# A transformer block on one core: the six middle batches of the attention stage written out one by one, instead of a loop on the engines

## The chip, the core and the metric

The kernel runs on one core of a Trainium2 chip. The metric is the device time of one execution, in microseconds. Five engines work on their own instruction streams and meet at semaphores: TensorE (PE: matmuls, with their weight loads as PEld), VectorE (DVE), ScalarE (ACT), GpSimd (POOL) and SyncE (SP), which here only starts transfers.

## What is computed

A "macaron" block: half of a mixture-of-experts layer, causal attention, and half of the same mixture again, each on a normalised input and added to x.

```
x = x + 0.5 * ffn(layernorm(x))       # x: 8 batches x 1024 tokens x 256
x = x + attn(layernorm(x))            # 16 heads of 16, causal softmax, output projection + bo
x = x + 0.5 * ffn(layernorm(x))
# ffn: top-2 of 8 experts per token; an expert whose count exceeds its capacity of 1280
#      tokens is dropped as a whole, and its tokens get nothing from it
```

The kernel works out the gate and the counts, and enters the expert code (`moe_experts`, from L527) only if an expert is within its capacity. In the trace it is jumped over both times, so both ffn parts come down to gates and counts.

## The kernel before

**Stages.** A short stage computes gates and counts for all 8192 tokens (to 94 us of the span). Then comes attention, to 1534 us, batch after batch, and behind it the second count.

**The attention of a batch** is four steps, one for each group of four heads (`hg` 0 to 3). A step runs over 12 groups of keys and queries with 4 heads each, 48 units. Per unit PE makes one transposed score tile (`st`, L1146), ACT takes its exponential into `probs` (L817), POOL masks the diagonal ones (`affine_select`, L668), and PE multiplies `probs` with the values into `o_bank` (`pv`, L1178). Beside that, 15 units ahead, the row maxima of the next step are found: PE makes score tiles in the other orientation (`s`, L1159) in three PSUM banks in turn, and DVE reduces each one. A tile on the diagonal is reduced together with the causal mask by `tensor_tensor_reduce` (L966, two instructions on DVE: the operation and the read of its accumulator into `max_diag`), a full one by `tensor_reduce` (`max_full`, L970). PE may write a bank again only when `max_done` says that DVE has taken its maximum. The maxima are split into three bf16 parts (`mfin`, L977 to L987, each after a drain), transposed by PE (L1131) and copied by ACT into `q_stack` (L804).

**Around the units** lies other work at fixed unit numbers (`PLACE`, a table written by hand): projections for later steps (`misc`, L1104, with a split into three bf16 parts by ACT, POOL and DVE), values (L1099), transposes of outputs, output projection (L1125), normalisation of the next batch's x (`lnstat` L449, `lnnorm` L458) and the gate of the last one. SP writes the parts to DRAM and reads them back as stacks.

**The order.** `step_plan` makes one list of events, and each engine's program goes through the same list and emits what is its own. The lists are in five sections (`make_sections`): prologue, batch 0, batches 1 to 6, batch 7, epilogue. `walk` (L269) goes through them. A section that occurs once is written out with constants. The section that occurs six times (`times` is 6) is emitted once inside `eng.Fori`, a loop that runs on each engine with the batch number `b` in a register, and the count that a wait compares with is then worked out from the register: `lin(b, k, c)` is `b * k + c`, and `n(...)` does the same for counts of a kind of event.

```
with eng.Fori(b0, b0 + times) as b:
    events(b)
```

**The increments.** `passed(eng, name)` (L438) follows certain waits on SP, POOL and DVE. It increments a semaphore that nobody waits for:

```
eng.wait_ge(s_full, lin(b, NU * NG, NU * (hg + ahead) + u + 1))
if diag:
    passed(eng, "vector")
```

The wait is then carried by the instruction that increments, and the operation comes behind it.

## Time and profile before

| | |
|---|---|
| median of three runs | 1573.51 us (1569.27 to 1577.14) |
| the profiled execution, its own time | 1577.63 us |
| its span, from first to last instruction | 1575.9 us |
| gates and counts, to | 94 us |
| prologue (maxima and projections of batch 0) | 94 to 183 us |
| batch 0, written out | 183 to 327 us |
| batches 1 to 6, looped | 327 to 1376 us |
| batch 7, written out | 1376 to 1534 us |
| epilogue and second count | to 1576 us |
| mean granted clock of TensorE | 0.936 of full speed |
| busy share | PE 85%, DVE 72%, ACT 62%, POOL 26% |

The profile is of one execution, 4.1 us above the median. PE's clock is granted at full speed (2.4 GHz, written 1.00) or at half of it (1.2 GHz); a window's figure between 0.5 and 1 is the mean of the two. "Idle before <-" names what ended an engine's wait. "issue" is idle time that no semaphore ended.

### The profile page before, as it was taken

What the parts mean: (1) busy time and instruction counts of PE and PEld (TensorE: products, weight loads), DVE (VectorE), ACT (ScalarE), POOL (GpSimd) and SP (SyncE); (2) the same over time, 40 slices, a digit from 0 to 9 for tenths busy, and PEclk for the clock granted to TensorE, in tenths of its full rate; (3) what the DMA queues carried; (4) which work ended last, traced back from release to release, by engine and by line L of the source; (5) the groups of instructions that cost most, each with busy time, mean ns of one, the idle gap of its engine ahead of it and who ended that gap; (6) DMA issues with size and microseconds to landing.
All of it is one profiled execution on the core that took longest, in us unless ns stands there. A gap on an engine that the chain in (4) does not pass through costs nothing.

```text
span 1575.9 us, 32770 instructions
## 1 busy us (share of the span) xinstructions
PE 1344.9 (85%) x8464; PEld 581.0 (37%) x8464; DVE 1127.1 (72%) x3677; ACT 977.3 (62%) x1729; POOL 413.3 (26%) x536
## 2 busy tenths in 40 slices
PE   3645799999988899989988898989998998999874
PEld 2422233344433443344333343344433443344332
DVE  6723788777876778767877777767886777768642
ACT  5411377766666667756666767757765766666751
POOL 2311223223321232223321232223322232222110
PEclk9866799999998999999999999999999999999985
DMA  7022412222322222312322232202322232221000
GB/s 243 1 46 60 112 35 61 61 61 61 81 59 63 46 59 72 74 33 61 88 59 55 53 82 62 62 26 61 88 61 53 60 80 61 63 53 40 5 1 27
DMA packets 53969, 95.75 MB, mean 61 GB/s; under 512 B 5776, under 2 KB 47376, under 8 KB 47632
## 3 DMA queue, kind: packets, MB, share of 16 engines
q1 hardware_dynamic: 51744, 92.29, 23.5%
q8 instruction: 83, 1.36, 0.4%
q10 hardware_dynamic: 2032, 1.19, 0.3%
q14 instruction: 110, 0.90, 0.2%
HBM read 59.91 MB, written 33.55 MB: 59 GB/s over the span
## 4 chain that ended last, share of the span: by engine, by line
PE 61%; DVE 12%; issue 11%; ACT 9%; DVEq 3%; DMA 2%; POOL 2%; ACTq 0%; SPq 0%; POOLq 0%
PE o_bank L1178 15%; PE s L1159 14%; PE st L1146 12%; PE misc L1104 7%; PE misc L1125 4%; PE misc L1099 3%; ACT q_stack L804 3%; PE misc L510 3%; DVE s L966 3%; ACT probs L817 2%; DVE max_full L970 2%; ACT parts L780 1%; DVE stats L449 1%; DVE xn L458 1%; DMA part_dram<-parts 1%
## 5 line engine op out<-in xcount | busy, mean ns | idle before, releaser
L817 ACT ACTIVATE probs<-st 128x512 f32<-128x512 f32 (+1 forms) x1216 | 632.3, 580 | 248.6 <-PE st L1146 128.5
L966 DVE CUSTOM_DVE_ANT_0 s<-s,causal 128x128 f32<-128x128 f32 (+3 forms) x1024 | 494.8, 504 | 239.3 <-PE s L1159 221.1
L1159 PE MATMUL s<-k_stack,q_stack 96*128 96x512 bf16 (+3 forms) x1536 | 507.6, 341 | 58.2 <-DVE max_diag L966 32.8
L1146 PE MATMUL st<-q_stack,k_stack 108*128 108x512 bf16 (+3 forms) x1536 | 499.8, 338 | 37.9 <-ACT probs L817 19.6
L970 DVE TENSOR_REDUCE max_full<-s 128x1 f32<-128x512 f32 x512 | 350.1, 684 | 32.5 <-PE s L1159 32.1
L1178 PE MATMUL o_bank<-probs,v_aug 128*17 128x512 f32 (+3 forms) x3072 | 332.7, 506 | 16.5 <-ACT parts L780 10.7
L668 POOL TENSOR_SCALAR_AFFINE_SELECT probs<-probs 128x512 f32<-128x512 f32 x256 | 164.6, 645 | 584.7 <-ACT probs L817 584.1
L1159 PEld LDWEIGHTS s<-k_stack,q_stack 96*128 96x128 bf16 x1536 | 150.4, 99 | 446.6 <-DVE max_diag L966 200.7
L1146 PEld LDWEIGHTS st<-q_stack,k_stack 108*128 108x128 bf16 x1536 | 151.2, 99 | 158.9 <-ACT probs L817 67.2
L804 ACT ACTIVATE q_stack<-misc 12x2048 bf16<-12x2048 f32 x64 | 119.7, 1870 | 77.4 <-PE misc L1131 76.7
L680 POOL TENSOR_TENSOR rest<-qk,parts 128x512 f32<-128x512 f32 x64 | 74.1, 1159 | 356.4 <-ACT parts L780 347.0
L1104 PE MATMUL misc<-x_t,w_qk 128*128 128x512 f32 x256 | 132.1, 641 | 21.9 <-issue 13.4
L966 DVE DVE_READ_ACCUMULATOR2_ANT max_diag<- 128x1 f32 x1024 | 144.3, 141 | 0.2
L780 ACT ACTIVATE qk<-misc,qk_bias,qk_scale 128x512 f32<-128x512 f32 x64 | 49.8, 777 | 139.2 <-PE misc L1104 123.7
L1178 PEld LDWEIGHTS o_bank<-probs,v_aug 128*17 128x17 f32 x3072 | 51.4, 96 | 142.4 <-issue 97.5
L686 POOL TENSOR_TENSOR parts<-rest,parts 128x512 bf16<-128x512 f32 x64 | 74.7, 1167 | 58.0 <-DVE parts L1010 58.0
L449 DVE BATCH_NORM_STATS2 stats<-x_all 128x6 f32 (+1 forms) x184 | 72.3, 419 | 10.5 <-issue 5.2
L458 DVE TENSOR_SCALAR xn<-x_all,mean_var,rstd 128x256 f32 (+1 forms) x152 | 64.1, 439 | 16.3 <-POOL rstd L465 13.8
L1104 PEld LDWEIGHTS misc<-x_t,w_qk 128*128 128x128 f32 x256 | 48.9, 202 | 64.4 <-issue 47.6
L1125 PE MATMUL misc<-w_o,o_t 128*128 128x256 f32 x256 | 67.2, 408 | 5.2 <-ACT parts L780 4.2
L1099 PE MATMUL misc<-w_v,x_t 128*128 128x256 f32 x256 | 65.0, 399 | 4.7 <-ACT parts L780 2.6
L1028 DVE TENSOR_TENSOR x_all<-misc,x_all 128x512 f32 (+1 forms) x32 | 22.1, 692 | 51.2 <-PE misc L1125 51.2
(107 smaller groups left out, 931.9 us busy)
## 6 DMA issues: line engine op xcount, KB each, us to landing
part_dram<-parts SPq DMA_DIRECT2D x128, 192.0 KB, 2.8
q_stack<-part_dram SPq DMA_DIRECT2D x32, 384.0 KB
k_stack<-part_dram SPq DMA_DIRECT2D x32, 384.0 KB
x_all<-x SPq DMA_DIRECT2D x16, 512.0 KB, 5.7
q_stack<-part_dram SPq DMA_DIRECT2D x32, 256.0 KB
k_stack<-part_dram SPq DMA_DIRECT2D x32, 256.0 KB
out<-x_all SPq DMA_DIRECT2D x8, 1024.0 KB, 17.1
q_stack<-part_dram SPq DMA_DIRECT2D x32, 128.0 KB
```

The source lines that it names most:

```text
L449: nc.vector.bn_stats(stats[:, t, :], x_tiles(tile, 1)[:, 0, :])
L668: nc.gpsimd.affine_select(out=now, in_=now, compare_op=ALU.is_ge, fill=0.0, base=0, pattern=[[0, HG], [1, P]], channel_multiplier=-1)\
L804: nc.scalar.activation(q_stack[rows, hm, :, c * CW:(c + 1) * CW], misc[rows, :].rearrange("p (o c) -> p o c", o=1) .to_broadcast([MROWS, H ...
L817: nc.scalar.activation(probs[:, g % 2, h - part:h + 1, 0:width], st_bank[i % 3][:, 0:share * width] .rearrange("p (h c) -> p h c", c=width ...
L966: nc.vector.tensor_tensor_reduce(out=bank, in0=bank, in1=causal[:, CW - width:CW], scale=1.0, scalar=-BIG, op0=ALU.add, op1=ALU.max, accum ...
L970: nc.vector.tensor_reduce(max_full[:, (hg + ahead) % 2, h, ib - CT:ib - CT + 1], bank, AX.X, ALU.max)\
L1099: last = nc.tensor.matmul(misc[:, t * D:(t + 1) * D], x_t[:, dc, t0:t0 + P], w_v[:, dc, :], start=dc == 0, stop=dc == DC - 1)
L1104: last = nc.tensor.matmul(misc[:, :], w_qk[:, dc, hq, :], x_t[:, dc, c * CW:(c + 1) * CW], start=dc == 0, stop=dc == DC - 1)
L1125: last = nc.tensor.matmul(misc[:, t * D:(t + 1) * D], o_t[:, dc, t * P:(t + 1) * P], w_o[:, dc, :], start=dc == 0, stop=dc == DC - 1)
L1146: score = nc.tensor.matmul(st_bank[i % 3][:, part * width:(part + 1) * width], k_stack[0:KROWS + MROWS, hg, h, jb * P:(jb + 1) * P], q_sta ...
L1159: nc.tensor.matmul(s_bank[u % 3][:, 0:width], q_stack[0:KROWS, hm, h, ib * P:(ib + 1) * P], k_stack[0:KROWS, hm, h, j0:j0 + width], start= ...
L1178: last = nc.tensor.matmul(o_bank[32 * h:32 * h + VW, off:CW], v_aug[:, jb, of % NG * HG + h, :], probs[:, g % 2, h, 0:CW - off], start=g i ...
```

## The change

`walk` loses the loop. It calls `handle` for batches 1, 2, ... 6 in turn, and passes an integer for `b` and an integer for each count. So `lin` and `n` give constants, slices of `x_all` and `out` that depended on `b` are fixed, and a wait carries its number. All waits remain, with the same values at each event. Second, the increments in the attention stage go: five calls of `passed` on SP and POOL and the one on DVE. Those in the loads, the first normalisation and the expert code remain, as do the small loop of the gate stage and the branches over the experts. No operation on data is added, removed or moved.

```diff
-def walk(eng, handle):
+def walk(handle):
     for plan, times, b0, start in SECTIONS:
-        def events(b):
-            seen = dict.fromkeys(start, 0)
+        for i in range(times):
+            seen = {k: start[k] + i * count(plan, k) for k in start}
             for hg, kind, *a in plan:
                 def n(k, more=0):
-                    if times == 1:
-                        return start[k] + seen[k] + more
-                    per = count(plan, k)
-                    return b * per + (start[k] + seen[k] + more - per * b0)
-                handle(b, n, hg, kind, *a)
+                    return seen[k] + more
+                handle(b0 + i, n, hg, kind, *a)
                 if kind in seen:
                     seen[kind] += 1
-        if times == 1:
-            events(b0)
-        else:
-            with eng.Fori(b0, b0 + times) as b:
-                events(b)
...
                     eng.wait_ge(part3_ready, lin(b, 2 * m[0], 2 * m[1] + c + 1))
-                    passed(eng, "sync")
...
                         for half in range(2):
                             eng.wait_ge(parts_out[half], lin(b, 32 * m[0], 32 * m[1] + 32))
-                            passed(eng, "sync")
...
                     eng.wait_ge(misc_free, n("use", 1))
-                    passed(eng, "sync")
...
                         eng.wait_ge(exp_done, lin(b, NSB * NG, NSB * hg + exps_through(g)))
-                        passed(eng, "gpsimd")
...
                     eng.wait_ge(stats_ready, n("lnaggr", 1))
-                    passed(eng, "gpsimd")
...
                     eng.wait_ge(s_full, lin(b, NU * NG, NU * (hg + ahead) + u + 1))
-                    if diag:
-                        passed(eng, "vector")
```

In the orders below a row "ISA" or "REGISTER_ALU" without names is an instruction on a register; waits that stand alone are not shown. The changed file has its own line numbers: L1130 is L1146 of before, L1143 L1159, L1162 L1178, L1103 L1119, L950 L966, L954 L970, L440 L449.

PE where one looped batch ends, before: the last rows of the loop body and its jump.

```order
L1146 MATMUL st<-q_stack,k_stack 128x128
L294 ISA
L1159 MATMUL s<-k_stack,q_stack 128x512
L1146 MATMUL st<-q_stack,k_stack 128x128
L294 ISA
L1159 MATMUL s<-k_stack,q_stack 128x512
L287 REGISTER_ALU
L287 COMPARE_AND_BRANCH
```

From there PE goes back to the head of the body, where the next batch starts:

```order
L287 ISA
L294 ISA
L1146 MATMUL st<-q_stack,k_stack 128x512
L1174 ISA
L1178 MATMUL o_bank<-probs,v_aug 17x256 x4
L294 ISA
L1159 MATMUL s<-k_stack,q_stack 128x512
L294 REGISTER_ALU
```

The same place in the changed program, batch 1 going over into batch 2:

```order
L1143 MATMUL s<-k_stack,q_stack 128x384
L1130 MATMUL st<-q_stack,k_stack 128x128
L1143 MATMUL s<-k_stack,q_stack 128x512
L1130 MATMUL st<-q_stack,k_stack 128x128
L1143 MATMUL s<-k_stack,q_stack 128x512
L1130 MATMUL st<-q_stack,k_stack 128x128
L1143 MATMUL s<-k_stack,q_stack 128x512
L1130 MATMUL st<-q_stack,k_stack 128x512
L1162 MATMUL o_bank<-probs,v_aug 17x256 x4
L1143 MATMUL s<-k_stack,q_stack 128x512
L1130 MATMUL st<-q_stack,k_stack 128x512
L1143 MATMUL s<-k_stack,q_stack 128x512
```

The old batch ends with the fourth `L1143` row, and the new one starts with the `L1130` row of 128x512 behind it. The comparison, the jump and the register rows are gone; the matmuls stand in the same order. Every engine has such a jump before, and none has it now.

DVE in step 0 of a looped batch, where maxima alternate with `lnstat`, before:

```order
L970 TENSOR_REDUCE max_full<-s 128x1
L961 ISA
L966 ISA s,max_diag<-s,causal 128x128
L966 ISA max_diag 128x1
L449 ISA
L449 BN_STATS stats<-x_all 128x6
L961 ISA
L970 TENSOR_REDUCE max_full<-s 128x1
L449 ISA
L449 BN_STATS stats<-x_all 128x6
L961 ISA
L966 ISA s,max_diag<-s,causal 128x256
```

and now:

```order
L954 TENSOR_REDUCE max_full<-s 128x1
L950 ISA s,max_diag<-s,causal 128x128
L950 ISA max_diag 128x1
L440 BN_STATS stats<-x_all 128x6
L954 TENSOR_REDUCE max_full<-s 128x1
L440 BN_STATS stats<-x_all 128x6
L950 ISA s,max_diag<-s,causal 128x256
L950 ISA max_diag 128x1
```

The register rows of L961 and L449 (the address of the x tile) go, and the operations keep their order. The increments (L438) are of a kind that is not shown here: 386 instructions of the built program for DVE wait and increment before, and 2 now.

## Rows read from the trace of the kernel before

**Rows 1.** The page: busy time by engine, then the chain that ended last by engine.

```profile
PE 1344.9 (85%) x8464; PEld 581.0 (37%) x8464; DVE 1127.1 (72%) x3677; ACT 977.3 (62%) x1729; POOL 413.3 (26%) x536
...
PE 61%; DVE 12%; issue 11%; ACT 9%; DVEq 3%; DMA 2%; POOL 2%; ACTq 0%; SPq 0%; POOLq 0%
```

**Rows 2.** Waits of PE in batch 2: who, ended by whom, us in total, times, longest.

```profile
PE st L1146 <- issue: 3.6, 1, 3.6
PE s L1159 <- DVE max_diag L966: 3.4, 7, 0.7
...
PE s L1159 <- DVE max_full L970: 0.9, 2, 0.5
```

**Rows 3.** Chain of waits where batch 2 begins: start us, us, what.

```profile
499.04 3.27 issue
```

**Rows 4.** Timeline of ACT there: start us, us, row, idle time before it.

```profile
504.09 0.60 ACT L817 ACTIVATE probs<-st 128x512 f32<-128x512 f32 x1 [5.06 <-PE o_bank L1178]
```

**Rows 5.** Windows across the starts of batches 1 to 7, and the columns of windows.

```profile
core 0: us, PE busy (x) PEld busy (x) DVE busy (x) ACT busy (x) POOL busy (x), PEclk, DMA share, GB/s
324.09:331.98 7.89, 6.86 (x55) 2.94 (x55) 6.91 (x26) 6.35 (x11) 1.86 (x3) 1.00 0.30 64
495.61:508.80 13.19, 9.37 (x56) 3.73 (x56) 7.73 (x26) 5.52 (x8) 1.86 (x3) 0.74 0.17 55
671.41:683.26 11.85, 8.28 (x56) 3.62 (x55) 7.58 (x25) 5.41 (x8) 1.86 (x3) 0.86 0.18 59
846.57:858.70 12.13, 8.25 (x55) 3.34 (x55) 6.90 (x25) 5.67 (x9) 1.52 (x3) 0.86 0.18 55
1021.27:1034.46 13.19, 9.37 (x56) 3.73 (x56) 7.73 (x26) 5.52 (x8) 1.86 (x3) 0.74 0.17 54
1197.08:1209.17 12.09, 8.28 (x55) 3.69 (x55) 7.37 (x25) 5.41 (x8) 1.68 (x3) 0.86 0.18 56
1372.82:1380.63 7.81, 6.86 (x56) 2.92 (x56) 6.79 (x26) 6.01 (x10) 1.86 (x3) 1.00 0.20 56
```

**Rows 6.** Windows of whole batches: batches 1 and 6.

```profile
327.20:502.30 175.10, 158.77 (x1011) 68.22 (x1011) 133.54 (x438) 117.44 (x209) 50.20 (x62) 0.97 0.26 63
...
1203.80:1376.10 172.30, 160.15 (x1011) 68.96 (x1011) 130.82 (x429) 117.03 (x208) 47.92 (x59) 0.96 0.25 61
```

**Rows 7.** Windows of step 1 of batch 2 (looped) and of batch 7 (written out).

```profile
552.70:595.10 42.40, 41.61 (x266) 20.02 (x264) 31.97 (x100) 28.70 (x54) 14.65 (x16) 1.00 0.32 78
1420.10:1459.20 39.10, 37.90 (x258) 18.76 (x257) 31.49 (x98) 25.38 (x50) 10.01 (x13) 1.00 0.12 42
```

**Rows 8.** The same window of batch 2, for L1104 alone.

```profile
552.70:595.10 42.40, 3.92 (x8) 1.37 (x8) 1.00 0.32 78
```

**Rows 9.** Timeline of PE: two score matmuls for which DVE waits.

```profile
510.69 0.22 PE L1159 MATMUL s<-k_stack,q_stack 96*128 96x128 bf16 x1
...
525.09 0.38 PE L1159 MATMUL s<-k_stack,q_stack 96*128 96x512 bf16 x1
```

**Rows 10.** Timeline of DVE: the two maxima that follow them.

```profile
511.10 0.30 DVE L966 CUSTOM_DVE_ANT_0 s<-s,causal 128x128 f32<-128x128 f32 x1 [0.91 <-PE s L1159]
...
525.51 0.69 DVE L970 TENSOR_REDUCE max_full<-s 128x1 f32<-128x512 f32 x1 [0.34 <-PE s L1159]
```

**Rows 11.** Waits of DVE in batch 2.

```profile
DVE s L966 <- PE s L1159: 27.7, 28, 4.4
...
DVE stats L449 <- issue: 0.9, 4, 0.2
```

**Rows 12.** Waits of PE in the whole run, for comparison with rows 2.

```profile
PE s L1159 <- DVE max_diag L966: 32.8, 77, 0.8
```

**Rows 13.** The page: instructions; packets of the queues that carry code, MB, share.

```profile
span 1575.9 us, 32770 instructions
...
q8 instruction: 83, 1.36, 0.4%
...
q14 instruction: 110, 0.90, 0.2%
```

More of the change, by code:

```diff
@@ L607, in _ @@
             moe_sync(0)
-            walk(eng, handle)
+            walk(handle)
             eng.wait_ge(out_written, 16 * B)
@@ L699, in _ @@
             moe_pool(0)
-            walk(eng, handle)
+            walk(handle)
             moe_pool(1)
@@ L829, in _ @@
             eng.wait_ge(bias_scaled, 1)
-            walk(eng, handle)
+            walk(handle)
             moe_scalar(1)
@@ L1034, in _ @@
             moe_vector(0)
-            walk(eng, handle)
+            walk(handle)
             eng.wait_ge(misc_free, COUNTS_AFTER["use"] + 1)
@@ L1188, in _ @@
             eng.wait_ge(weights_in, 16 * WEIGHT_DMAS)
-            walk(eng, handle)
+            walk(handle)
             moe_tensor(1)
```

## The prediction

> **What bounds the kernel now.** I read the page first, then the waits of PE in one looped batch, then what happens where one looped batch follows another, and at last windows of equal work inside the loop and outside it. TensorE is busy 85% of the span and holds 61% of the chain that ended last; DVE holds 12%, and 11% is "issue", time in which nothing that the profile shows was waited for [rows 1]. So the question is not how many instructions go, but where PE stood still because of them. In batch 2 PE's largest single wait is one of 3.6 us with "issue" as its end. Its waits for DVE's maxima are small and several: 3.4 us in 7 and 0.9 us in 2 [rows 2]. The change can act on these two kinds: it removes the jump back, and it takes instructions off the way between PE and DVE.
>
> **The jump back.** Where batch 2 begins, the chain has 3.27 us of "issue" between the end of the last exponential and the first score matmul of the new batch [rows 3]. No engine's work ends that wait. ACT stands still longer: its first exponential starts at 504.09, after 5.06 us [rows 4], though the matmul that feeds it started at 502.31 (3.27 behind 499.04) and needs some 0.6 us. So each engine takes its own pause at the jump, and ACT's ends last. To price this I take the same work across all seven batch starts, from the last transpose of maxima (L1131) in the old batch to the first value matmul (L1099) in the new one [rows 5]. Batch 1 is entered from above and batch 7 by falling out of the loop, so neither start has a jump back: 7.89 and 7.81 us. The five with one take 13.19, 11.85, 12.13, 13.19 and 12.09. Against 7.89 that is 5.30 + 3.96 + 4.24 + 5.30 + 4.20 = 23.0 us. It is more than five stalls of 3.6 us (18.0). The rest, 5.0, is ACT's late start and the clock: the granted clock is 1.00 in the two windows without a jump and 0.74 to 0.86 in the five with one, so PE fell to 1.2 GHz for a part of each after it had stood still [rows 5]. Without the stall this goes too. The DMA share and the work counts of these windows differ little, and the two starts without a jump differ by 0.08 us, so I trust the 23.0 to about a microsecond.
>
> The Trainium skill (Advanced Engine Details and Errata, section Control Flow Timing) puts a compare-and-branch at about 108 ns. By that figure five jumps would cost 0.5 us, and the sum below would lose 22.5 us of its gain. Rows 3 and 5 show some thirty times as much here, and the measurement decides.
>
> **What of it is given back.** A batch that starts earlier does not always end as much earlier. Batch 1, which has no jump at its start, took 175.1 us with the stall of 3.6 at its end, so 171.5 without, and six such batches take 1029.0. The six took 1048.9 (327.2 to 1376.1) [rows 6]. That is a gain of 19.9, 3.1 less than 23.0; the mean clock of batch 1 is 0.97 and that of batch 6, which has a jump ahead of it, 0.96, so the half-speed stretches elsewhere in a batch do not go. I take 2 us as given back, between 0 and 3.1.
>
> **Register instructions before waits.** Where PE is the bound, they cost nothing. Step 1 of batch 2 takes 42.4 us and the same step of batch 7, written out with constants, 39.1 [rows 7]. The lists of the two differ by a projection: L1104 has 8 matmuls, 3.92 us busy, in the first [rows 8] and none in the second. The difference in time, 3.3, is less than that, and PE's busy time differs by 3.7. So 0 here, hidden behind 41.6 us of matmuls; without that cover they would be on the sequencers' way between two operations. On ACT, POOL and SP the same: each waits longer for others than the instructions take, and PE's waits for ACT have the length of whole exponentials. No transfer is moved: SP issues the same ones in the same order, only without an increment ahead.
>
> **The way between PE and DVE.** A score matmul starts at 510.69 and takes 0.22 us, so it ends at 510.91 [rows 9]. The maximum on the diagonal behind it starts at 511.10, 0.19 later [rows 10]. For a full tile the matmul ends at 525.47 [rows 9] and the maximum starts at 525.51, 0.04 later [rows 10]. The difference, 0.15 us, is the increment, which holds the wait while the operation comes behind it. With the wait in the operation I expect 0.04 in both. DVE waited in this way 28 times in batch 2 [rows 11], but most of that is idle time of an engine that is not the bound. It counts where PE then waits for the maximum: 7 times a batch [rows 2], 7 x 0.15 = 1.05 us. The register row ahead of each `lnstat` adds "issue" on DVE of 0.9 us a batch in 4 pieces [rows 11], in a burst in which PE waits for DVE; I count a fifth, 0.15. That makes 1.2 us a looped batch, 7 us for six. The bounds are 0 and all that PE waits for the maxima, 3.4 + 0.9 = 4.3 a batch or 26 us. I stay near the lower one because DVE is backlogged before several of these waits, and then a shorter way to its start changes nothing.
>
> Outside the loop only the increments go. PE waits 77 times for a maximum on the diagonal in the whole run [rows 12], of which 6 x 7 = 42 in the loop, so 35 outside: at most 35 x 0.15 = 5 us, at least 0. Here too DVE is often backlogged, and part of it lies in the prologue beside transfers: I take 1.5.
>
> **The sum.** 23.0 - 2 + 7 + 1.5 = 29.5 us less. The profiled execution took 1577.6 us, which gives 1548.1. It lies 4.1 us above the median of the runs shown; against that median the same sum gives **1544.0**, a gain of 1.9%. A measurement of this kernel can tell about 0.5%, some 8 us, from no change.
>
> **Rivals.** (1) Only the jumps pay. DVE is backlogged wherever PE waits for it, and 3 us are given back: a gain of 20, so 1553.5. For it: the waits for DVE come in bursts. Against it: the 0.15 us is on the way 28 times a batch. (2) Much more inside the batches: with a wait no longer held by an instruction that only the sequencer handles, DVE can line up its next operations earlier, and half of the bound goes too: 23 + 13 + 4 = 40 less, 1533.5. For it: the "issue" before `lnstat`. Against it: step 1, which shows nothing. (3) The jump is cheap and the pause at it is a wait for something else that also comes without the jump, a stack or an engine that is behind. Then writing the batches out only renames it, and 7 + 1.5 remain: 1565.0; with these absent too it is no change. This is what the change not doing what it says would look like. The figure of 108 ns would speak for it. Against it: the starts of batches 1 and 7 need the same things and have no pause [rows 5].
>
> (4) Slower: the fetch of the code. Written out, the body of the loop stands six times in memory, and each engine reads all of it. If reading on made PE pause at every packet of code, the 83 packets of the queue with the larger ones [rows 13] would have to cost 29.5 / 83 = 0.36 us each to use up the gain, and 0.45 to make it 8 us slower; at 0.5 each the time is 1585. Against it: the queues already moved 2.26 MB of code in 193 packets in this run [rows 13]. The profile counts 32,770 executed instructions [rows 13], which makes 69 bytes for each, so the loop was already read again in each pass, and the amount will fall, not grow. And batch 7, written out, runs step 1 with only 39.1 - 37.9 = 1.2 us outside PE's busy time [rows 7]. The Trainium skill (Runtime: NRT & Kernel Launch, section Instruction fetch mechanics) says that fetching ahead is purely sequential and that the cost of passing on to the next block is mostly hidden, while a jump out of the blocks held must wait for a fetch. By that page this rival has no price; the trace agrees as far as batches 0 and 7 show.
>
> **How the numbers follow.** Forecast as summed, 1538 to 1550: 0.58. Rival 1: 0.22. Rival 2: 0.10. Rival 3: 0.06, a good half of it within 0.5%. Rival 4: 0.04, most of it slower. The range reaches from a little beyond rival 2 to beyond rival 1, since the median of new runs may also lie as the profiled one does, 4 us higher: 1530 to 1560, with about 0.1 left out above and 0.05 below. Faster by over 0.5%: 0.92. Within: 0.05. Slower: 0.03.
>
> **What would show it.** In the new profile no wait of 3 us with "issue" on PE at the starts of batches 2 to 6, a granted clock of 1.00 in the same windows, and 7.6 to 7.9 us from L1131 to L1099 at each. ACT's first exponential follows its matmul at once. Looped batches of 175 us become 170 to 171. The start of a diagonal maximum stands 0.04 us behind its matmul, and PE's waits for `max_diag` shrink by about a third. The packets of code are no more than before. I am wrong if a pause remains at the starts (rival 3), if new waits with "issue" lie scattered over PE's timeline (rival 4), or if the batches end up at 172 (rival 1) or 168 (rival 2).

## The result, and the profile after

| | before | after |
|---|---|---|
| median | 1575.33 us (1569.27 to 1578.09) | 1512.59 us (1509.79 to 1514.33) |
| ratio | | 0.9606, 95% interval 0.9585 to 0.9627 |
| the profiled execution | 1577.63 us | 1511.56 us |
| start of batch 0 | 182.7 | 181.0 |
| batch 0 | 144.5 | 142.0 |
| batches 1 to 6 | 1048.9 | 992.1 |
| batch 7 to the end of the span | 199.8 | 194.7 |

The change takes 62.7 us off the median, 3.9%. The forecast was 29.5, and its range ended at 1530.0. The last four rows are of the profiled executions, where a batch goes from its first score matmul (`st`) to that of the next. Of the 66.1 us between the two spans (1575.9 and 1509.8), 56.8 lie in the six batches that were a loop (9.5 each) and 9.3 outside them.

The page of the changed kernel: instructions, busy time, the two queues that carry code, and the chain that ended last. They answer to [rows 1, 13].

```profile
span 1509.8 us, 25323 instructions
...
PE 1301.3 (86%) x8464; PEld 569.6 (38%) x8464; DVE 1122.5 (74%) x3677; ACT 975.7 (65%) x1729; POOL 412.8 (27%) x536
...
q8 instruction: 67, 1.10, 0.3%
...
q14 instruction: 60, 0.49, 0.1%
...
PE 58%; ACT 15%; DVE 14%; issue 5%; POOL 3%; DMA 2%; DVEq 2%; SPq 0%; POOLq 0%; ACTq 0%
```

The counts of operations on data are those of before, to the last one; 7,447 instructions that the profile counts as none are gone. "issue" fell from 11% to 5% of the chain. The code moved fell from 193 packets to 127: it is longer in memory and yet is fetched less.

Windows across four of the starts of batches 1 to 7, from the last transpose of maxima to the first value matmul, as in [rows 5] (the other three are like the first within 0.01 us):

```profile
320.09:327.35 7.26, 6.67 (x54) 2.73 (x52) 6.48 (x23) 5.88 (x10) 1.75 (x3) 1.00 0.30 67
484.79:492.05 7.26, 6.67 (x54) 2.73 (x52) 6.49 (x23) 5.88 (x10) 1.75 (x3) 1.00 0.19 55
980.99:988.60 7.61, 6.67 (x55) 2.73 (x53) 6.59 (x24) 6.23 (x11) 1.86 (x3) 1.00 0.18 55
1312.20:1319.46 7.26, 6.67 (x54) 2.73 (x52) 6.48 (x23) 5.88 (x10) 1.75 (x3) 1.00 0.19 50
```

The five starts that took 11.85 to 13.19 us take 7.26 or 7.61, at the full clock. The chain of waits at the start of batch 2 no longer has the 3.27 us of "issue" of [rows 3]:

```profile
485.04 1.87 ACT q_stack L790
486.91 0.02 issue
486.94 0.61 ACT probs L803
487.54 0.06 issue
```

ACT goes from the copy into `q_stack` straight to the exponential. Whole batches (1 and 6, as [rows 6]), then step 1 of batch 2 and of batch 7 (as [rows 7]):

```profile
323.00:487.70 164.70, 153.48 (x1011) 67.22 (x1011) 131.66 (x435) 117.10 (x209) 48.90 (x61) 0.99 0.27 65
1150.50:1315.10 164.60, 152.22 (x1011) 66.90 (x1011) 131.36 (x435) 116.84 (x209) 48.97 (x61) 1.00 0.27 65
```

```profile
533.20:574.70 41.50, 40.95 (x265) 19.95 (x264) 32.51 (x100) 28.36 (x55) 14.18 (x16) 1.00 0.33 82
1358.80:1397.60 38.80, 37.79 (x256) 18.60 (x257) 31.54 (x98) 25.33 (x50) 9.97 (x13) 1.00 0.13 42
```

A batch without a jump at its start takes 164.7 where it took 175.1, with 3.6 us of stall at its end; so some 6.8 us a batch went that have nothing to do with a jump. Step 1 lost 0.9 us in batch 2, and 0.3 in batch 7, where only increments went.

All six batches as one window, before and after:

```profile
327.20:1376.10 1048.90, 957.23 (x6062) 411.00 (x6061) 792.82 (x2595) 703.19 (x1249) 294.09 (x361) 0.96 0.25 62
```

```profile
323.00:1315.10 992.10, 924.36 (x6061) 404.65 (x6061) 789.34 (x2595) 702.24 (x1249) 293.48 (x361) 0.99 0.27 65
```

Of the 56.8 us that they lost, 32.9 are busy time of PE and 23.9 its idle time. A part of the busy time is the clock: by the trace's record PE had the lower of its two levels (1.2 GHz) for some 75 us of these batches before and for some 27 after.

PE's waits in batch 2, and over the whole run, as [rows 2, 12]:

```profile
PE s L1143 <- DVE max_diag L950: 2.4, 4, 0.8
...
PE s L1143 <- DVE max_full L954: 1.0, 2, 0.5
```

```profile
PE s L1143 <- DVE max_diag L950: 23.8, 49, 0.9
```

The waits for a maximum on the diagonal fell from 77 with 32.8 us to 49 with 23.8.

A score matmul and the maximum on the diagonal that waits for it, from the timelines of PE and of DVE, as [rows 9, 10]:

```profile
495.66 0.23 PE L1143 MATMUL s<-k_stack,q_stack 96*128 96x128 bf16 x1
```

```profile
495.93 0.30 DVE L950 CUSTOM_DVE_ANT_0 s<-s,causal 128x128 f32<-128x128 f32 x1 [0.65 <-PE s L1143]
```

495.66 + 0.23 = 495.89, and the maximum starts 0.04 us later, where it had been 0.19. That was forecast.

**The way between two operations of DVE.** The timeline shows what the totals don't. The same two operations in step 0 of batch 2, the CAST of the remainders and the maximum on the diagonal behind it, first of before, then of after. DVE is backlogged here: neither row has an idle time before it.

```profile
508.66 0.17 DVE L985 CAST max_parts<-max_rest 128x16 bf16<-128x16 f32 x1
508.93 0.30 DVE L966 CUSTOM_DVE_ANT_0 s<-s,causal 128x128 f32<-128x128 f32 x1
```

```profile
492.88 0.18 DVE L969 CAST max_parts<-max_rest 128x16 bf16<-128x16 f32 x1
492.96 0.29 DVE L950 CUSTOM_DVE_ANT_0 s<-s,causal 128x128 f32<-128x128 f32 x1
```

From start to start it is 0.27 us before and 0.08 after. The maximum now begins before the end of the CAST is reported; before, it began 0.10 us behind it. So these two ran 0.19 us further apart although the matmul's result was there, and that is the row which the prediction lacks.

The CAST is short. Behind a longer operation of a backlogged DVE nothing changed. Step 2 of batch 2, first of before, then of after:

```profile
602.70 0.42 DVE L449 BATCH_NORM_STATS2 stats<-x_all 128x6 f32 x1
603.03 0.28 DVE L966 CUSTOM_DVE_ANT_0 s<-s,causal 128x128 f32<-128x128 f32 x1
```

```profile
581.78 0.42 DVE L440 BATCH_NORM_STATS2 stats<-x_all 128x6 f32<-128x256 f32 x1
582.11 0.28 DVE L950 CUSTOM_DVE_ANT_0 s<-s,causal 128x128 f32<-128x128 f32 x1
```

0.33 us from start to start in both. Counted over the six batches, 168 of the 768 maxima on the diagonal stand behind one of the short operations (0.17 us) that split the maxima into parts, and their median start moved from 0.09 us behind the reported end to 0.09 ahead of it. Some 400 more have their matmul's result in time and a longer operation, or the read of the accumulator, ahead of them. Most of these start 0.08 or 0.14 us ahead of its end, in both kernels. The others wait for PE.

### The profile page after: what moved, and what is told of

Same layout as the page of the kernel before. It is cut to its first block, busy times and chain, and to the rows that moved or that the text cites. A ratio compares the mean times of both kernels' runs of the same rounds, so it can differ in the third digit from the quotient of the medians.

```text
span 1509.8 us, 25323 instructions
## 1 busy us (share of the span) xinstructions
PE 1301.3 (86%) x8464; PEld 569.6 (38%) x8464; DVE 1122.5 (74%) x3677; ACT 975.7 (65%) x1729; POOL 412.8 (27%) x536
## 4 chain that ended last, share of the span: by engine, by line
PE 58%; ACT 15%; DVE 14%; issue 5%; POOL 3%; DMA 2%; DVEq 2%; SPq 0%; POOLq 0%; ACTq 0%
PE o_bank L1162 14%; PE s L1143 12%; PE st L1130 11%; PE misc L1088 7%; ACT q_stack L790 5%; DVE s L950 4%; ACT probs L803 4%; PE misc L1109 4%; PE misc L1083 3%; PE misc L501 3%; DVE max_full L954 2%; ACT parts L766 2%; ACT qk L766 2%; DMA part_dram<-parts 1%; DVE o_tok L1001 1%
## 5 line engine op out<-in xcount | busy, mean ns | idle before, releaser
L950 DVE CUSTOM_DVE_ANT_0 s<-s,causal 128x128 f32<-128x128 f32 (+3 forms) x1024 | 493.8, 502 | 184.1 <-PE s L1143 179.9
L1143 PE MATMUL s<-k_stack,q_stack 96*128 96x512 bf16 (+3 forms) x1536 | 496.6, 335 | 54.9 <-DVE max_diag L950 23.8
L1130 PE MATMUL st<-q_stack,k_stack 108*128 108x512 bf16 (+3 forms) x1536 | 490.5, 332 | 21.0 <-ACT probs L803 18.6
L954 DVE TENSOR_REDUCE max_full<-s 128x1 f32<-128x512 f32 x512 | 349.9, 683 | 39.8 <-PE s L1143 38.3
L1162 PE MATMUL o_bank<-probs,v_aug 128*17 128x512 f32 (+3 forms) x3072 | 325.6, 496 | 19.3 <-ACT parts L766 9.2
L1143 PEld LDWEIGHTS s<-k_stack,q_stack 96*128 96x128 bf16 x1536 | 149.5, 98 | 413.2 <-DVE max_diag L950 179.8
L1130 PEld LDWEIGHTS st<-q_stack,k_stack 108*128 108x128 bf16 x1536 | 150.1, 99 | 142.6 <-ACT probs L803 63.8
L950 DVE DVE_READ_ACCUMULATOR2_ANT max_diag<- 128x1 f32 x1024 | 144.0, 141 | 0.0
L1162 PEld LDWEIGHTS o_bank<-probs,v_aug 128*17 128x17 f32 x3072 | 51.2, 95 | 145.0 <-issue 85.6
L440 DVE BATCH_NORM_STATS2 stats<-x_all 128x6 f32<-128x256 f32 (+1 forms) x184 | 72.1, 418 | 6.9 <-DVE mean_var L445 2.9
L449 DVE TENSOR_SCALAR xn<-x_all,mean_var,rstd 128x256 f32<-128x256 f32 (+1 forms) x152 | 61.8, 424 | 16.2 <-POOL rstd L456 13.4
L1083 PE MATMUL misc<-w_v,x_t 128*128 128x256 f32 x256 | 60.9, 380 | 3.6 <-ACT v_aug L756 2.1
L994 DVE CAST parts<-rest 128x512 bf16<-128x512 f32 x64 | 35.5, 555 | 29.3 <-POOL rest L666 29.3
## 6 DMA issues: line engine op xcount, KB each, us to landing
out<-x_all SPq DMA_DIRECT2D x8, 1024.0 KB, 17.5
```

The source lines that it names most:

```text
L950: nc.vector.tensor_tensor_reduce(out=bank, in0=bank, in1=causal[:, CW - width:CW], scale=1.0, scalar=-BIG, op0=ALU.add, op1=ALU.max, accum ...
L954: nc.vector.tensor_reduce(max_full[:, (hg + ahead) % 2, h, ib - CT:ib - CT + 1], bank, AX.X, ALU.max)\
L1083: last = nc.tensor.matmul(misc[:, t * D:(t + 1) * D], x_t[:, dc, t0:t0 + P], w_v[:, dc, :], start=dc == 0, stop=dc == DC - 1)
L1130: score = nc.tensor.matmul(st_bank[i % 3][:, part * width:(part + 1) * width], k_stack[0:KROWS + MROWS, hg, h, jb * P:(jb + 1) * P], q_sta ...
L1143: nc.tensor.matmul(s_bank[u % 3][:, 0:width], q_stack[0:KROWS, hm, h, ib * P:(ib + 1) * P], k_stack[0:KROWS, hm, h, j0:j0 + width], start= ...
L1162: last = nc.tensor.matmul(o_bank[32 * h:32 * h + VW, off:CW], v_aug[:, jb, of % NG * HG + h, :], probs[:, g % 2, h, 0:CW - off], start=g i ...
```

## The experiments

All differences are of medians, on the same chip as a run of the kernel before. "Registers" is short for counts and addresses worked out from the loop's register.

### Increments alone: everything written out with constants, all increments kept

`walk` is that of the change, and every `passed(...)` of before stays.

```diff
-            with eng.Fori(b0, b0 + times) as b:
-                events(b)
+        for i in range(times):
+            seen = {k: start[k] + i * count(plan, k) for k in start}
```

> The six batches written out with constants as in the change, but all increments of the kernel before kept. It separates the increments from the rest. Against the changed kernel (1512.6 us): theory I (the increment that holds the wait is what was undersized) says 15 to 25 us slower, so 1528 to 1538, because batch 0, which was written out in both kernels and lost only increments, got 2.5 us shorter (144.5 to 142.0), and eight such batches make 20. The rival, that the increments matter for a microsecond per batch at most and the rest came from jumps and registers, says at most 8 us slower, 1513 to 1521. In batch 0, both say 144.5 us again.

Measured: 1527.76 us (1523.98 to 1530.57), ratio 0.9686 (0.9648 to 0.9723). The increments are worth 15.2 us; the other 47.5 of the 62.7 belong to the loop, its jumps and its registers together. The changed kernel and this one come from different sets of runs. By the ratios, each against the kernel before of its own set, the increments are worth 12.6 us, and either figure is uncertain by some 6.

### One jump in place of five

```diff
-            with eng.Fori(b0, b0 + times) as b:
-                events(b)
+            with eng.Fori(0, 2) as i:
+                for j in range(times // 2):
+                    events(i * (times // 2) + (b0 + j))
```

> The kernel before with its loop of six passes made a loop of two passes over three batches: one jump back instead of five, the batch number still in a register in every batch, all increments kept. It prices four jumps alone. If a jump costs what stands between L1131 and L1099 (4.6 us each, the forecast), 18.4 us are gained: 1557. If a jump also brings on later half-speed stretches inside its batch, it costs 7 to 8 us and the time is 1543 to 1547. If the registers bring on those stretches, batches without a jump still take 171 us and show them in the granted clock, and the time is 1557.

Measured: 1557.61 us (1555.68 to 1559.52), ratio 0.9881 (0.9846 to 0.9915). Windows across the start of batch 3, which has no jump here, and of batch 4, which has the only one:

```profile
666.85:674.58 7.73, 6.53 (x55) 2.76 (x52) 6.70 (x24) 6.05 (x10) 1.85 (x3) 1.00 0.19 63
836.87:849.98 13.11, 9.16 (x55) 3.55 (x52) 7.50 (x25) 5.49 (x8) 1.86 (x3) 0.74 0.16 55
```

So the pause and the half-speed clock behind it belong to the jump. Four jumps fewer give 17.5 us on one chip and in one set of runs: 4.4 each, 21.9 for five. The register instructions of this version are a little longer (medians of 55 ns in place of 37 on PE and of 69 in place of 46 on DVE), so that is if anything too low, and what follows for the registers too high. What is left between this kernel and the first experiment, with the same increments, is 29.85 us; less one jump, **25.5 us are the registers**, for which the forecast had 0. The clock has little part in it: in the six batches PE had its lower level for 41 us here and for 37.5 in the first experiment.

### PE alone written out, and PE alone looped

PE alone written out: the block of PE calls `walk_out`, which is the written-out `walk`, and the other four the loop. PE alone looped: the other way round. All increments are kept in both.

```diff
-            walk(eng, handle)
+            walk_out(handle)
```

> PE alone goes through the six batches written out, with constants and without a jump; the other four engines keep the loop, its registers and jumps; all increments kept. Against the kernel before (1575 us). Two effects of PE's own are switched off: its register rows and its pause at the jump. If the 25 us that jumps and increments leave unexplained sit on PE's instruction stream, most of them are gained here, and of the 22 us of the jumps only a part, because ACT still pauses over 5 us: 1575 - 22 - 5 = 1548, within 1542 to 1554. If they sit on DVE or ACT, the kernel stays within 10 us of before: 1565 to 1575, and the starts of batches 2 to 6 still show the 3 to 5 us, now as a wait for ACT.

> The converse: PE alone keeps the loop with registers and jumps, the other four are written out with constants; all increments kept. If the register rows cost on PE, this one has PE's whole stall of 3.6 us at five starts and PE's rows: 5 us of ACT's share of the jumps are gained and little more, 1565 to 1572. If they cost on DVE and ACT, 25 us and more are gained: 1540 to 1550.

Measured: PE alone written out 1565.55 us (1557.93 to 1568.40), ratio 0.9938 (0.9911 to 0.9965); PE alone looped 1550.66 us (1546.31 to 1555.44), ratio 0.9844 (0.9817 to 0.9872). Step 1 of batch 2, of the first and of the second:

```profile
551.00:593.30 42.30, 41.52 (x266) 19.71 (x264) 31.88 (x100) 28.57 (x54) 14.59 (x16) 1.00 0.31 80
```

```profile
544.00:585.90 41.90, 41.35 (x265) 20.03 (x264) 32.46 (x100) 28.60 (x55) 14.35 (x16) 1.00 0.32 81
```

With no register instruction on PE the step takes what it took before (42.40); with all of them on PE and none elsewhere it takes what it takes in the first experiment (540.3 to 582.2, 41.9). So PE's own cost nothing that shows in this step; those of the other engines cost 0.4. The two gains, 9.8 and 24.5 by their ratios, do not add up to the 49 of the first experiment, for a jump left on either side keeps a pause at each start. Where batch 2 begins, the PE that has no jump waits for an ACT that has one:

```profile
PE st L1159 <- ACT probs L830: 3.2, 1, 3.2
```

### Which engine's increments

The kernel after the change with DVE's increment back; in the other run POOL's two.

```diff
                     eng.wait_ge(s_full, lin(b, NU * NG, NU * (hg + ahead) + u + 1))
+                    if diag:
+                        passed(eng, "vector")
```

> The changed kernel (1512.6 us) with the increments on DVE alone put back, 1024 of them. Keeping all increments costs 15.2 us. If DVE's way from PE is the place, nearly all of it comes back: 1522 to 1528. If the others (POOL's between exponential and mask, SP's ahead of the transfers) carry half, 1518 to 1521.

> The changed kernel with the increments on POOL alone put back, 286 of them. The forecast took them as nothing, since POOL waits for ACT over 500 us and PE seldom waits for POOL. By that it stays within 2 us of 1512.6. If the mask is on PE's way to the values matmuls, 3 to 8 us slower: 1516 to 1521. Together with the run with DVE's increments it should make at most 15.

Measured: DVE's increments back 1533.66 us (1533.30 to 1536.17), ratio 0.9751 (0.9730 to 0.9772): 21 us more than the changed kernel. POOL's back 1510.64 us (1507.55 to 1515.70), ratio 0.9600 (0.9569 to 0.9631): nothing that can be told. PE does wait a little more for POOL's maskings (9.3 us in the run in place of 7.2), and less for `max_diag` (20.5 in place of 23.8). It is DVE's that cost.

But DVE's alone cost 6 us more than all of them together in the first experiment, so one more run had DVE's and POOL's, without SP's:

> The kernel after the change with the increments of DVE and of POOL back, SP's left out: e1_const_inc without SP's. e5_dve_inc (DVE's alone) took 1533.7 and e1_const_inc (all) 1527.8, 6 us less with more instructions. If POOL's increments, by making the maskings later, shift PE's order of waiting to its good: 1526 to 1529. If it is SP's: 1532 to 1535. If 6 us are only what such kernels scatter by from one arrangement to another, anything from 1526 to 1536.

Measured: 1524.89 us (1522.08 to 1525.71), ratio 0.9670 (0.9632 to 0.9709). With POOL's beside them, DVE's cost 12 us, with SP's too 15, alone 21 (by the ratios 10, 13 and 23). So POOL's increments, worth nothing alone, give back 6 to 9 us where DVE has its own (by the ratios 10 to 13). PE's waits for `max_diag` say the same, here 33.2 us, with DVE's increments alone 37.2.

The traces show what differs on DVE. The same CAST of batch 2 and the masking of POOL beside it, first with DVE's increments alone, then with POOL's too (each fence has a row of DVE's timeline and one of POOL's):

```profile
617.81 0.64 DVE L967 CAST max_parts<-max_diag 128x16 bf16<-128x16 f32 x1
```

```profile
617.78 0.64 POOL L655 TENSOR_SCALAR_AFFINE_SELECT probs<-probs 128x512 f32<-128x512 f32 x1 [2.43 <-ACT probs L803]
```

```profile
612.53 0.17 DVE L969 CAST max_parts<-max_diag 128x16 bf16<-128x16 f32 x1
```

```profile
612.60 0.63 POOL L656 TENSOR_SCALAR_AFFINE_SELECT probs<-probs 128x512 f32<-128x512 f32 x1 [2.53 <-ACT probs L805]
```

Where the masking starts 0.03 us ahead of the CAST, the CAST takes 0.64 us, to the masking's end; where it starts 0.07 behind, 0.17. Of the 256 short operations that split the maxima, 75 take over 0.23 us with DVE's increments alone and 30 in this run and in the first experiment, and every one of them overlaps an operation of POOL. Together the 256 take 73.2 us and 56.2. That is 17 us of DVE for some 9 of the whole. It fits, but no run shifts the maskings alone with DVE's increments in place, so it is not shown that this is all of it. The term is 12 to 21 us, by what else stands in the program.

### Which engine's registers

The first experiment's kernel (constants, all increments), with one or two engines on registers, in two passes of three batches and thus with one jump.

`walk_reg` is the loop of two passes of above.

```diff
-            walk(handle)
+            walk_reg(eng, handle)
```

> As e1_const_inc (1527.8 us: written out, constants, all increments), but DVE alone computes its waits in registers, in a loop of two passes over three batches with one jump. The same for all five engines, e2_one_jump, took 1557.6, so 29.8 us lie between, of which the one jump is about 4 and the register instructions the rest. Theory A: the register instructions cost on DVE, whose answer to each score matmul PE needs: 1545 to 1555, nearly all of it. Theory B: they cost on ACT, whose evictions and exponentials feed PE: this run stays within 5 us of 1527.8. Theory C: every engine's share is small and they add up: some 1535.

> As e7_dve_reg, with ACT in place of DVE as the one engine that computes its waits in registers and has the one jump. Theory A (DVE): within 5 us of 1527.8, the jump of ACT included. Theory B (ACT): 1545 to 1555. Theory C: some 1535. ACT's probs instructions would begin 0.10 us behind the matmul that they wait for, as in the loop of before, in place of 0.02.

> As e7_dve_reg, with DVE and ACT both computing their waits in registers in two passes, and PE, POOL and SP written out. If the cost lies on these two alone, this is e2_one_jump again, 1553 to 1558, whatever their shares. If POOL and SP have a share (POOL's masking of the exponentials starts 0.10 us later with a register), some 5 us less, 1548 to 1552. If the sum of e7 and e8 over e1 is well above this, the two hide behind each other.

| on registers, one jump | median | ratio | over the first experiment |
|---|---|---|---|
| DVE | 1549.78 us (1547.85 to 1551.41) | 0.9861 (0.9827 to 0.9895) | 22.0 |
| ACT | 1541.38 us (1541.28 to 1541.55) | 0.9811 (0.9779 to 0.9844) | 13.6 |
| DVE and ACT | 1556.36 us (1553.47 to 1558.48) | 0.9903 (0.9867 to 0.9939) | 28.6 |
| all five | 1557.61 us (1555.68 to 1559.52) | 0.9881 (0.9846 to 0.9915) | 29.9 |

The first experiment and that with all five on registers come from another set of runs, in which the kernel before took 1575.09 us; beside these three it took 1570.79. By the ratios each of the three lies 5 to 6 us further from the first experiment. The profiled executions side with the medians: batches 1 to 6 take 1003.3 us in the first experiment, 1021.6 with DVE on registers, 1014.0 with ACT, 1030.7 with both and 1030.3 with all five. I go by the medians, and some 5 us are uncertain in each.

DVE and ACT on registers are as slow as all five, so PE, POOL and SP add nothing that can be told. Each row holds one jump, and I take 4.4 off for it, though that was measured with all engines jumping. It can't be far off: in the profiled executions the batch that begins with the jump is 3.9, 4.7 and 3.6 us longer than the mean of the other five. So DVE's are worth 17.6 us, ACT's 9.2, both 24.2: they add up nearly, 26.8 against 24.2. None of the three theories was wholly right: DVE has the larger part, ACT a real one.

On DVE the pair of above shows it again; of the first experiment, then with DVE on registers:

```profile
499.58 0.17 DVE L976 CAST max_parts<-max_rest 128x16 bf16<-128x16 f32 x1
499.76 0.30 DVE L957 CUSTOM_DVE_ANT_0 s<-s,causal 128x128 f32<-128x128 f32 x1
```

```profile
504.75 0.18 DVE L999 CAST max_parts<-max_rest 128x16 bf16<-128x16 f32 x1
505.04 0.30 DVE L980 CUSTOM_DVE_ANT_0 s<-s,causal 128x128 f32<-128x128 f32 x1
```

0.18 us with the increment, 0.29 with register and increment, against 0.08 with neither. PE's waits over the whole run follow, in the same order:

```profile
PE s L1150 <- DVE max_diag L957: 33.3, 83, 0.9
```

```profile
PE s L1173 <- DVE max_diag L980: 43.5, 115, 1.5
```

On ACT it is another place. Step 0 of batch 2, PE's group of eight value matmuls and ACT's exponential that waits for it; first the first experiment, then ACT on registers (each fence shows a row of PE's timeline and one of ACT's):

```profile
540.61 0.63 PE L1169 MATMUL o_bank<-probs,v_aug 128*17 128x256 f32 x8
```

```profile
541.30 1.11 ACT L808 ACTIVATE probs<-st 128x512 f32<-128x512 f32 x2 [0.43 <-PE o_bank L1169]
```

```profile
542.82 0.63 PE L1192 MATMUL o_bank<-probs,v_aug 128*17 128x256 f32 x8
```

```profile
543.62 1.08 ACT L831 ACTIVATE probs<-st 128x512 f32<-128x512 f32 x2 [0.53 <-PE o_bank L1192]
```

540.61 + 0.63 = 541.24, and the exponential starts 0.06 later; 543.45, and it starts 0.17 later. The register instruction carries the wait, and the exponential comes behind it. ACT waited so 16 times in batch 2:

```profile
ACT probs L831 <- PE o_bank L1192: 11.3, 16, 1.2
```

16 x 0.11 x 6 batches = 10.6 us, near the 9.2 measured. PE needs these exponentials soon, so here nearly the whole of each tenth arrives at the end.

### A register instruction alone, used for nothing

The kernel after the change, with this in the block of DVE:

```diff
+                    if 1 <= b < B - 1:
+                        eng.reg_mul(base, base, 3)
+                        eng.reg_add(base, base, u)
                     eng.wait_ge(s_full, lin(b, NU * NG, NU * (hg + ahead) + u + 1))
```

The two calls become one instruction.

> The kernel after the change (1512.6 us), with one register instruction whose result nothing uses ahead of each of the 1158 maxima of the six middle batches on DVE; the waits stay constants held by the operations, and no increment comes back. Theory A: the cost found on DVE in e7_dve_reg (22 us with one jump, some 17 without) is that of the instruction itself, which stands between two operations of DVE: 1525 to 1530. Theory B: it costs only together with a wait that something other than the operation holds (register or increment); alone it is done while DVE still computes: 1511 to 1515.

Measured: 1516.71 us (1515.02 to 1518.46), ratio 0.9622 (0.9585 to 0.9660). That is 4.1 us more (2.5 by the ratios), with intervals that overlap, and about a quarter of what DVE's registers cost. The pair:

```profile
494.52 0.18 DVE L972 CAST max_parts<-max_rest 128x16 bf16<-128x16 f32 x1
494.68 0.30 DVE L953 CUSTOM_DVE_ANT_0 s<-s,causal 128x128 f32<-128x128 f32 x1
```

0.16 us, twice the 0.08 of the changed kernel: behind a short operation the instruction is not hidden. Its effect on PE is small all the same:

```profile
PE s L1152 <- DVE max_diag L953: 26.3, 55, 1.1
```

Theory B holds better than A: the instruction by itself is mostly done while DVE computes. What costs comes with its use, in a wait that the register instruction or the increment carries, or in an operation that needs its result; these were not told apart.

### A version beyond the change: the stage of the gates written out too

```diff
-            with eng.Fori(1, NCH // LOADS) as four:
+            for four in range(1, NCH // LOADS):
```

The loop of the loads on SP and that of the first normalisation on POOL become such loops of Python too, without their increments.

> The kernel after the change with the stage ahead of the batches (normalising, transposes and gate logits of all chunks) written out too, on all engines, and its increments on SP and POOL dropped. If its jumps and registers cost as those of the batches do, a jump every four chunks and 1 to 2 us each: 5 to 15 us less than the changed kernel, 1498 to 1508. If the stage is bound by DVE's normalising or by the loads of x, which none of this shortens: 1510 to 1513, no change. If the larger code in its place makes the first run through it wait for code: 1515 or more.

Measured: 1508.65 us (1505.59 to 1509.06), ratio 0.9596 (0.9563 to 0.9629), against 0.9606 (0.9585 to 0.9627) of the change. The stage itself became shorter. The first projection, in the chain of waits of the change and of this run:

```profile
93.83 1.19 PE misc L1088
```

```profile
88.66 1.19 PE misc L1086
```

Of these 5.2 us, 2.4 are left where batch 0 starts (178.6 in place of 181.0), and batch 7 to the end of the span takes 1.8 us more (196.5 in place of 194.7). In the whole run the difference can't be told from none. In the stage PE waits as long for DVE's `xn` as before (26.0 us and 25.9); what took back the rest was not followed further.

## Why the prediction was wrong in size

**The jumps: right.** "23.0 - 2" stood for 21; four jumps taken out gave 17.5, so five 21.9. All that was named is seen: no "issue" of 3 us, the clock at 1.00 in the same windows, ACT's exponential at once. The 7.6 to 7.9 us from transposes to values became 7.26, and the batches 164.7 in place of 170 to 171, since they hold the other terms too. One reason was wrong: "the half-speed stretches elsewhere in a batch do not go". Of the 75 us at the lower clock in the six batches, 24 lay in the five windows at the starts; with four jumps fewer 41 of the 75 are left, after the change 27. Batch 1, which begins without a jump in both, has a mean clock of 0.99 in place of 0.97.

**"Register instructions before waits. Where PE is the bound, they cost nothing": this step failed, and with it 25 us.** Two things were wrong in it. First, the subtraction. Step 1 of batch 2 against step 1 of batch 7 differed by 3.3 us, L1104 was 3.92 us busy, and so nothing was left [rows 7, 8]. But both steps are written out now, and they differ by 41.5 - 38.8 = 2.7 us: that is what the projection costs, with whatever else only batch 2 does there (ACT is busy 3.0 us more in it and POOL 4.2). The busy time of some matmuls is not what the step would lose without them. The 0.9 us that the step lost (some 0.5 by the registers, 41.9 in the first experiment, and the rest by the increments) were covered by this. Second, and worth more, the reach: step 1 is the one in which PE waits least (0.8 us of 42.4), and its result was carried over to the rest of the batch, and from PE to DVE and ACT with "each waits longer for others than the instructions take". That an engine waits long says nothing for an instruction that comes behind the wait. On PE they do cost nothing that can be told. On ACT they stand between the matmul and the exponential (0.17 against 0.06 us), on DVE between a short operation and the next.

**The way between PE and DVE: mechanism right, size wrong.** The forecast had 7 us in the loop and 1.5 outside; with the increments of all engines it is 15.2, with DVE's alone 21. The step that mis-sized it is "DVE is backlogged before several of these waits, and then a shorter way to its start changes nothing". It holds behind longer operations, where nothing changed, and fails behind the short ones of the split: there a backlogged DVE gained more (0.19 us from start to start) than where it waits for PE (0.15). I had only measured the second case, and counted its 7 waits a batch. There are 28 maxima a batch behind a short operation; at 0.18 us that is 30 us of DVE in the six batches, for increments and registers together, and what of it arrives at the end is argued, not measured. Even the upper bound of 26 us, "all that PE waits for the maxima", was not wide enough as a bound of the whole. PE still waits 23.8 us for them, 9.0 less than before, while increments and registers are worth 40.7; most of the gain came from time that these waits did not hold.

**The rivals.** Rival 2 had the mechanism, that an increment or register instruction which holds the wait keeps the next operation from being lined up, and it was given 0.10 and 40 us. "Against it: step 1, which shows nothing" leaned on the same faulty subtraction. Rivals 1 and 3 are refuted by the first two experiments, rival 4 by the page: fewer packets of code, less "issue".

**Given back:** 2 us were taken off for starts that come earlier and end less so. No run separates that.

**The sum as it came out:** jumps 21.9, registers 25.5 (DVE 17.6, ACT 9.2, both together 24.2), increments 15.2, together 62.6 of 62.7. It closes by the way it is made, as a chain of kernels from before to after; only the split among engines is measured apart from it, and the fifth jump is put at the price of the other four. In another order some us would shift between the terms, as the 12 to 21 us of DVE's increments show.

## What to carry to other kernels

Ask of each register instruction and each increment not how long it takes but where it stands: where it carries the wait for an operation that another engine needs, it delays that operation by a tenth or two each time. On a backlogged engine it is hidden behind a long operation (0.4 us here) and not behind a short one (0.17). Look at two neighbouring operations of the backlogged engine in the timeline: if the second starts behind the end of the first rather than a little ahead of it, something stands between them. And when a stretch is to show that something is free, take one where the engine in question is on the path, not one where another engine hides it.

## What was not expected of the hardware

**A backlogged DVE pays for what stands behind its short operations.** The same pair from start to start: 0.08 us with nothing between, 0.16 with a register instruction, 0.18 with an increment that holds the wait, 0.27 to 0.29 with both. The Trainium skill (Perfetto Trace Analysis, section Per-engine timelines) has the picture for it: an operation of DVE or ACT goes into a wait queue with its semaphores and leaves the sequencer free to decode the next, while an instruction that the sequencer does itself holds the sequencer until its own wait is over. The trace agrees: without increments the next operation starts 0.10 us before the reported end of the one ahead of it, and with an increment it starts 0.01 us behind it (499.58 + 0.17 against 499.76). Behind the 0.42 us of a BATCH_NORM_STATS2 neither register nor increment shows: 0.33 us from start to start with both and with neither.

**A short operation of DVE is stretched beside one of POOL.** A CAST of 0.17 us took 0.64 when POOL's masking had begun 0.03 us earlier, and 0.17 when the masking began 0.07 us later. So a tenth of delay on POOL, from increments that nobody waits for, can make DVE faster.

**A jump costs 4.4 us of the whole and slows the clock behind it.** The one window with a jump has a mean clock of 0.74, its neighbours 1.00, and PE had paused for some 3.6 us before. That the pause is a fetch of code fits the packets, of which 66 fewer were moved, but no run here shows which packet PE waited for.

**The clock goes with the jumps, not with the other two terms.** In batches 1 to 6 PE had the lower clock for some 75 us before, 41 with one jump, 37.5 in the first experiment and 27 after the change; a microsecond at half speed can cost at most half of one. So it can hold up to 17 us of what four jumps are worth, under 2 of the registers and up to 5 of the increments. With DVE's increments alone it is 20.5 us, less than in the changed kernel, and those batches take 12.6 us longer. What the jumps cost in clock is counted in their 4.4 us.

What couldn't be tried: a loop on registers without increments, since there the operations would have to wait on a register's value themselves. So the cost of registers is known only with increments beside it.
